# Random features of linear attention as two products of packed, rounded rows, and the second head's outputs behind the next pair's projections

## The chip, the core and the metric

One core of a Trainium2 chip runs the whole program. Its engines run side by side, each with its own queue of instructions: TensorE (PE in the rows; PEld is its weight load) multiplies, VectorE (DVE) and ScalarE (ACT) work element by element on SBUF and PSUM, GpSimd (POOL) and SyncE (SP) issue transfers. They meet at semaphores. The metric is the device time of one execution in microseconds, lower is better.

## The reference

A network of two layers on 1250 tokens of width 768: graph attention and linear attention side by side, then a feed-forward part. The change is in the linear attention, which each layer does once, with 12 heads of width 64. Layer 0 has 384 random features, another set `w` for each head, a bias on q, k and v, and a scale:

```python
def _feature_map(x, w):                       # layer 0, SCALE = 64 ** -0.25
    xs = x * SCALE
    proj = jnp.einsum('bhnc,hcm->bhnm', xs, w)
    sq = 0.5 * jnp.sum(xs * xs, axis=-1, keepdims=True)
    return jnp.exp(proj - sq) / np.sqrt(M)
...
q = _feature_map(qkv[0], w_orf)
k = _feature_map(qkv[1], w_orf)
D = jnp.einsum('bhnm,bhm->bhn', q, jnp.sum(k, axis=2))[..., None] + EPSILON
ktv = jnp.einsum('bhnm,bhnc->bhmc', k, v)
out = jnp.einsum('bhnm,bhmc->bhnc', q, ktv) / D
```

Layer 1 does the same with 256 features that all heads share, no bias and no scale.

## The kernel before

The program is a chain of stages. `performer_stage` is called twice, as `perf0` (layer 0, m = 384 features) and `perf1` (layer 1, m = 256). Tokens come in 10 tiles of 125, the 768 channels in 6 blocks of 128, the 12 heads in 6 pairs, so that a pair's q or k is one 128-row product: rows 0 to 63 are the first head (x = 0), rows 64 to 127 the second (x = 1). The input and the projection weights are split into a high part, rounded to the f32r format, and a rest in the same format; a projection is three f32r products per block (rest by high, high by rest, high by high, L592).

Before the change a pair goes so:

- TensorE projects q, then k (L592), in chunks of 512, 512 and 226 tokens into three PSUM banks. Every second pair it computes the values of two pairs first (L576).
- VectorE adds the bias and copies each chunk to SBUF, one copy per head (L732, without bias L735), and writes the squares of a head's 64 rows into the 64 rows of the other half of the same buffer (L742).
- The feature product (L605) is one plain fp32 product over 128 rows: 64 rows of q or k by the features, 64 rows of squares by the constant -0.5 times the scale. So exp needs no further term. These products go round five PSUM banks, and ScalarE empties them with exp (L672) into `qphi` and `kphi`.
- `k_t_v` (L630) sums kphi by v over the tokens, 65 columns wide with a column of ones for the denominator; VectorE copies the result (`keep_ktv`, L754). `outputs` (L643) is qphi by that, and VectorE divides (`keep_out`, L764 to L769) and SyncE stores.
- TensorE's order for heads 0 and 1: q(0), k(0), k(1), k_t_v(0), q(1), outputs(0), k_t_v(1), outputs(1). Then the next pair is projected.

The order is that of the code, engine by engine; no planner sets it. VectorE has further work in this stage: it splits the next weights (`split_w`, L706 and L708), and in `perf1` it scans one head of the graph attention per pair for its maxima (`MaxScan`, L1708, ten tiles of 125 x 1250), before it looks at the pair's `keep_ktv`. In `perf0` GpSimd adds the graph's edges to a matrix by 160 scattering transfers (L438), beside all this.

## Time and profile before

| | |
|---|---|
| time, median of 3 runs | 3726.37 us (3709.74 to 3729.12) |
| time of the profiled execution | 3719.97 us |
| its span | 3718.2 us |
| mean granted TensorE clock | 0.912 |
| TensorE busy | 3131.9 us, 84% of the span |
| VectorE busy | 2224.0 us, 60% |
| ScalarE busy | 1269.7 us, 34% |
| `perf0` | about 143 to 669 us of the span |
| `perf1` | about 2567 to 3009 us |

The span is what the trace covers; the execution's own time lies 1.8 us above it. The granted clock is the share of full speed that the chip allows TensorE: 1.00 is 2.4 GHz and 0.50 is 1.2 GHz. Matmuls are pipelined, so what one of them costs in a row of them is the distance from start to start, not the duration shown beside it. A plain fp32 product leaves two records in the trace.

### The profile page before, as it was taken

The page shows a single profiled execution, that of the slowest core. Times are in us where ns is not written, and L with a number is a line of the kernel's source. Part 1 is how long each engine was busy: PE and PEld are TensorE (multiplying, and loading weights), DVE is VectorE, ACT ScalarE, POOL GpSimd, SP SyncE. Part 2 cuts the span into 40 slices and gives each one's busy share as a digit, 9 for nine tenths or more (in the row PEclk, how much of TensorE's full clock was granted, in tenths as well). Part 3 has the DMA queues.
Part 4 walks back from the last instruction along what each step waited for, and adds up shares of the span by engine and source line. Part 5 has one row for each costly group of instructions (what it writes and reads, how often), then busy time and mean ns, then how long its engine had stood idle before and what let it go on. Part 6 is the DMA issues. An engine that isn't in the chain of part 4 may idle for free. (4 is left out here: it accounts for less than half of the span.)

```text
span 3718.2 us, 49900 instructions
## 1 busy us (share of the span) xinstructions
PE 3131.9 (84%) x18054; PEld 2553.8 (69%) x18054; DVE 2224.0 (60%) x3569; ACT 1269.7 (34%) x2193; POOL 452.4 (12%) x301
## 2 busy tenths in 40 slices
PE   8799999769899898786978499876999966886695
PEld 5678788655687898675977133356888844776694
DVE  6422222455670454996774788656654647996775
ACT  5341322213111332554133477521211211553245
POOL 0488860110000000000001400000000000000000
PEclk9799999889899999998989599878999988997897
DMA  6222220675420653422331211254111065214121
GB/s 200 56 28 23 24 20 8 194 221 132 107 61 29 175 157 94 125 74 82 76 76 26 82 39 47 60 176 125 39 40 41 14 170 155 70 43 119 47 51 43
DMA packets 253114, 311.06 MB, mean 84 GB/s; under 512 B 98898, under 2 KB 182455, under 8 KB 252297
## 3 DMA queue, kind: packets, MB, share of 16 engines
q1 hardware_dynamic: 178141, 276.25, 27.3%
q0 software_dynamic: 74784, 32.32, 4.9%
q8 instruction: 115, 1.88, 0.2%
q14 instruction: 74, 0.61, 0.1%
HBM read 226.94 MB, written 80.57 MB: 83 GB/s over the span
## 5 line engine op out<-in xcount | busy, mean ns | idle before, releaser
L438 POOL DMA_INDIRECT adj_d<-key_val,key_off x160 | 333.5, 2085 | 193.7 <-issue 166.7
L672 ACT ACTIVATE perf_qphi<-perf_wide,perf_lnm 128x512 f32<-128x512 f32 x180 | 102.9, 605 | 687.0 <-PE perf_wide L605 687.0
L2921 DVE TENSOR_TENSOR expert_wgel<-expert_gel,expert_wps 128x417 f32<-128x417 f32 (+1 forms) x384 | 201.7, 584 | 63.4 <-PE expert_wps L2846 57.8
L1909 PE MATMUL gat00att_ops<-gat00att_h,gat00att_p 125*125 x1600 | 197.3, 279 | 45.9 <-DVE gat00att_p L1885 45.9
L1909 PE MATMUL gat10att_ops<-gat10att_h,gat10att_p 125*125 x1600 | 194.4, 278 | 48.0 <-DVE gat10att_p L1885 47.9
L1909 PEld LDWEIGHTS gat00att_ops<-gat00att_h,gat00att_p 125*125 125x125 f32 x1600 | 183.1, 189 | 60.3 <-issue 60.1
L1909 PEld LDWEIGHTS gat10att_ops<-gat10att_h,gat10att_p 125*125 125x125 f32 x1600 | 182.4, 190 | 60.3 <-issue 60.3
L2893 ACT ACTIVATE expert_gel<-expert_hps 128x417 f32<-128x417 f32 (+1 forms) x384 | 193.5, 519 | 51.3 <-DVE expert_wgel L2921 42.3
L1212 PE MATMUL fc_ops<-fc_w_hi,fc_x_lo 128*125 128x384 f32 x480 | 164.7, 343 | 15.1 <-DVE fc_w_lo L1260 15.1
L1068 PE MATMUL fc_ps<-y_lo,fc_w_hi 128*128 128x512 f32 (+1 forms) x432 | 155.1, 359 | 19.4 <-DVE fc_w_lo L1110 19.4
L903 PE MATMUL proj_hps<-proj_w,proj_aT 128*125 128x384 f32 x480 | 164.3, 501 | 0.6 <-DMA proj_w<-in_L_mix_W_proj 0.3
L1212 PE MATMUL fc_ops<-fc_w_lo,fc_x_hi 128*125 128x384 f32 x480 | 164.1, 342 | 0.0
L592 PE MATMUL perf_wide<-y_lo,perf_qk_hi 128*128 128x512 f32 (+1 forms) x432 | 154.4, 358 | 10.8 <-DVE perf_v L721 10.8
L1212 PE MATMUL fc_ops<-fc_w_hi,fc_x_hi 128*125 128x384 f32 x480 | 163.5, 341 | 0.0
L1068 PE MATMUL fc_ps<-y_hi,fc_w_lo 128*128 128x512 f32 (+1 forms) x432 | 155.4, 360 | 0.0
L1068 PE MATMUL fc_ps<-y_hi,fc_w_hi 128*128 128x512 f32 (+1 forms) x432 | 155.4, 360 | 0.0
L592 PE MATMUL perf_wide<-y_hi,perf_qk_lo 128*128 128x512 f32 (+1 forms) x432 | 154.3, 357 | 0.0
L592 PE MATMUL perf_wide<-y_hi,perf_qk_hi 128*128 128x512 f32 (+1 forms) x432 | 154.1, 357 | 0.0
L2839 PE MATMUL expert_hps<-first_z,first_w 99*128 99x417 bf16 (+1 forms) x384 | 132.1, 348 | 24.0 <-SPq L2794 20.2
L643 PE MATMUL perf_o_ps<-perf_ktv,perf_qphi 128*125 128x65 f32 x1200 | 146.1, 286 | 5.9 <-DVE perf_ktv L754 5.9
L643 PEld LDWEIGHTS perf_o_ps<-perf_ktv,perf_qphi 128*125 128x125 f32 x1200 | 144.9, 202 | 7.6 <-issue 7.5
L1834 ACT ACTIVATE gat10att_e<-gat10att_e,a_s 125x1250 f32<-125x1250 f32 x80 | 107.0, 1338 | 103.8 <-DVE gat10att_e L1872 103.6
(465 smaller groups left out, 7814.8 us busy)
## 6 DMA issues: line engine op xcount, KB each, us to landing
fc_w<-in_L_mix_fc_w SPq DMA_DIRECT2D x96, 384.0 KB
adj_d<-edge_zero SPq DMA_DIRECT2D x4, 2734.4 KB
gat00proj_adj<-adj_d POOLq DMA_DIRECT2D x20, 546.9 KB, 6.9
gat00att_sh<-shift_d SPq DMA_DIRECT2D x16, 546.9 KB
gat10att_sh<-shift_d SPq DMA_DIRECT2D x16, 546.9 KB
perf_w<-in_L_mix_qkv_w SPq DMA_DIRECT2D x18, 384.0 KB
perf_w<-in_L_mix_W_qkv SPq DMA_DIRECT2D x18, 384.0 KB
attn_d<-perf_o SPq DMA_DIRECT2D x12, 560.0 KB
```

Of the source, the lines that this page charges most:

```text
L438: nc.gpsimd.indirect_dma_start(out=adj_flat[u], out_offset=bass.IndirectOffsetOnAxis(ap=key_off[:, c:c + 1], axis=0), in_=key_val[:, c:c + ...
L592: ins = pe.matmul(proj[:, c0:c0 + cn], qk_parts[wp][:, k, kb, :], y_parts[yp][:, kb, c0:c0 + cn], start=(kb == 0 and n == 0), stop=(kb == ...
L643: ins = pe.matmul(o_ps[0:TP, bank, (t - t0) * vw:(t - t0 + 1) * vw], qphi[:, x, mb, t * TP:(t + 1) * TP], ktv[:, x, mb, :], start=(mb == 0 ...
L672: act.activation(out, in_, ACT.Exp, bias=lnm[0:parts, 0:1], scale=scale).then_inc(exp_done, 1)
L903: ins = pe.matmul(hps[0:TP, t % 2, c * 512:c * 512 + 384], aT[:, t % 2, kb, :], w[:, kb, c * 384:(c + 1) * 384], start=(kb == 0), stop=(kb ...
L1068: ins = pe.matmul(ps[:, u, c0:c0 + cn], wp[:, u, kb, :], yT[yp][:, kb, c0:c0 + cn], start=(kb == 0 and n == 0), stop=(kb == KB - 1 and n = ...
L1212: ins = pe.matmul(ops[0:TP, t % 4, c * 512:c * 512 + half], xp[:, u, rows], wp[:, u, c * half:(c + 1) * half], start=(k == 0 and n == 0), ...
L1834: act.activation(e[:, s % RING, :], e[:, s % RING, :], ACT.Exp, bias=a_s02[:, bass.ds(hd, 1), s]).then_inc(e_done, 1)
L1909: ins = pe.matmul(ops[0:TP, u, b, t * w:(t + 1) * w], p[:, s, (t0 + t) * TP:(t0 + t + 1) * TP], h[:, s, bass.ds(hd, 1), :], start=(s == 0 ...
L2839: pe.matmul(hps[:, q % 3, 0:cn], w1[0:ZK, u, j * 128:(j + 1) * 128], z[0:ZK, u, c0:c0 + cn], start=True, stop=True).then_inc(h_done, 1)
L2893: act.activation(gel[:, q % 3, 0:cn], hps[:, q % 3, 0:cn], ACT.Gelu_apprx_tanh).then_inc(gel_done, 1)
L2921: dve.tensor_tensor(wgel[:, q % W, 0:cn], gel[:, q % 3, 0:cn], wps[:, q % 3, 0:cn], ALU.mult).then_inc(wgel_done, 1)
```

## The change

- The feature product becomes two f32r products into the same bank. The first has on its 128 rows the rounded q or k of a head (64 rows) and its rest (64 rows), against the rounded features on both halves (`wa`). The second has the rounded values again, against the rests of the features, and on the other 64 rows the summed squares, rounded, and their rests, against -0.5 (`wb`).
- The packed rows are made in two steps. ScalarE, `rounded`: per chunk two Identity instructions over 64 rows, each of which writes the rounded chunk twice, and four Squares over 32 rows. VectorE, `rests`: per chunk one add of the squares' halves over 96 rows, two subtractions over 64 rows, two casts and two subtractions over 32 rows. VectorE's old copies and squares go.
- Chunks are 418, 416 and 416 tokens. k is projected before q.
- TensorE's order becomes k(0), q(0), k_t_v(0), k(1), outputs(0), k_t_v(1), q(1), a wait for all exps of the pair, every second pair the values, the next pair's projections, and only then outputs(1).
- `kphi` and `qphi` hold one head instead of two, so ScalarE's exps of head 1 wait for k_t_v(0) and outputs(0), and those of the next pair for k_t_v(1) and outputs(1). Outputs start on a third of qphi.
- VectorE's order per pair: split the next weights, four scan tiles, `keep_ktv(0)`, perhaps a split, two scan tiles, `keep_out(0)`, four scan tiles, `keep_ktv(1)`, in `perf0` the features' split, perhaps the values, the next pair's `rests`, `keep_out(1)`.
- The loop does two turns of two pairs, and the last two pairs are written out behind it. Two small buffers of the graph attention are allocated later; their instructions stay the same.

```diff
     mb_n = m // 128
     per = 512 // m
     n_k = NT // per
     n_phi = n_k + 3 * mb_n
-    Q0, K0 = (0, n_k + n_phi), (3 * mb_n, n_phi)
+    units = 2 * n_phi
+    K0, Q0 = (0, n_phi), (n_k, n_phi + n_k)
+    cols = [(0, 418), (418, 416), (834, 416)]
+    widest = 418
     phi_banks = [3, 4, 0, 1, 2]
     ring = len(phi_banks)
...
+                    def feature_bank(j):
+                        if 2 <= j < ring:
+
+                            pe.wait_ge(lo_done, g * 6 + 3 + j - 1)
+                        elif j >= ring:
+                            pe.wait_ge(exp_done, g * units + j - ring + 2)
+                        return phi_banks[j % ring]
+
+                    def k_features(x):
+                        fw = x if per_head else 0
+                        for n in range(n_k):
+                            bank = feature_bank(K0[x] + n)
+                            for y in range(per):
+                                tile = slice((n * per + y) * TP, (n * per + y + 1) * TP)
+                                out = wide[0:TP, bank, y * m:(y + 1) * m]
+                                pe.matmul(out, ab[:, 0, x, 0, tile], wa[:, fw, :], start=True, stop=False)
+                                ins = pe.matmul(out, ab[:, 0, x, 1, tile], wb[:, x, :], start=False, stop=True)
+                            ins.then_inc(phi_done, 1)
+
+                    def q_features(x):
+                        fw = x if per_head else 0
+                        j = Q0[x]
+                        for c, (c0, cn) in enumerate(cols):
+                            if x == 0:
+                                pe.wait_ge(s_done, g * 6 + 3 + c + 3)
+                            for mb in range(mb_n):
+                                bank = feature_bank(j)
+                                f = slice(mb * 128, (mb + 1) * 128)
+                                pe.matmul(wide[:, bank, 0:cn], wa[:, fw, f], ab[:, 1, x, 0, c0:c0 + cn],
+                                          start=True, stop=False)
+                                pe.matmul(wide[:, bank, 0:cn], wb[:, x, f], ab[:, 1, x, 1, c0:c0 + cn],
+                                          start=False, stop=True).then_inc(phi_done, 1)
+                                j += 1
...
+                    if per_head:
+                        pe.wait_ge(feat_split, g + 1)
+
+                    pe.wait_ge(s_done, g * 6 + 5)
+                    k_features(0)
+                    q_features(0)
+                    k_t_v(0)
+                    k_features(1)
+                    outputs(0)
+                    k_t_v(1)
+                    q_features(1)
+                    if not last:
+                        pe.wait_ge(exp_done, g * units + units + 1)
+                        if u == 1:
+                            values(i + 1)
+                        project(g + 1, i + u, 1 - u)
+                    outputs(1)
...
-                        pe.wait_ge(feat_ld[u], i * 32 + 32)
-                        pe.wait_ge(square_done, g * 12 + 6)
-                        q_features(0)
-
-                        pe.wait_ge(square_done, g * 12 + 12)
-                        k_features(0)
-                        k_features(1)
-                        k_t_v(0)
-                        q_features(1)
-                        outputs(0).then_inc(o_done, 1)
-                        k_t_v(1)
-                        outputs(1).then_inc(o_done, 1)
...
+                    for side in range(2):
+                        for c, (c0, cn) in enumerate(cols):
+                            n = side * 3 + c
+                            act.wait_ge(proj_done, g * 6 + n + 1)
+
+                            def bias(k, r0, r1):
+                                return bpair[r0:r1, k, 1 - side:2 - side] if biased else 0.0
+
+                            for x in range(2):
+                                r0 = 64 * x
+                                act.activation(ab[r0:r0 + 64, side, x, :, c0:c0 + cn],
+                                               wide[r0:r0 + 64, c, 0:cn].unsqueeze(1).to_broadcast([64, 2, cn]),
+                                               ACT.Identity, bias=bias(0, r0, r0 + 64))
+
+                            act.wait_ge(s_done, g * 6 + n + 1)
+                            act.wait_ge(add_done, g * 6 + n + 1)
+                            for x in range(2):
+                                r0, to = 64 * x, slice(64 - 64 * x, 96 - 64 * x)
+                                act.activation(sq[to, n % 2, 0:cn], wide[r0:r0 + 32, c, 0:cn], ACT.Square,
+                                               bias=bias(1, r0, r0 + 32), scale=root)
+                                ins = act.activation(more[to, 0:cn], wide[r0 + 32:r0 + 64, c, 0:cn], ACT.Square,
+                                                     bias=bias(1, r0 + 32, r0 + 64), scale=root)
+                            ins.then_inc(sq_done, 1)
...
+                    def k_exps(x):
+
+                        act.wait_ge(ktv_done, g * 2 + x + 1)
...
+                    k_exps(0)
+                    q_exps(0)
+                    k_exps(1)
+                    q_exps(1)
+                    if not last:
+                        rounded(g + 1)
...
-                        q_exps(0)
-                        k_exps(0)
-                        k_exps(1)
-                        q_exps(1)
...
-                        for k, dest in enumerate((qs, ks)):
-                            for c, (c0, cn) in enumerate(CHUNKS):
-                                dve.wait_ge(proj_done, g * 6 + k * 3 + c + 1)
-                                for x in range(2):
-                                    rows = slice(64 * x, 64 * x + 64)
-                                    if biased:
-                                        ins = dve.tensor_scalar(dest[rows, x, c0:c0 + cn], proj[rows, c0:c0 + cn],
-                                                                bcols[rows, bass.ds(g + k * KB, 1)], None, ALU.add)
-                                    else:
-                                        ins = dve.tensor_copy(dest[rows, x, c0:c0 + cn], proj[rows, c0:c0 + cn])
-                                    ins.then_inc(plain_done, 1)
-
-                                dve.wait_ge(plain_done, g * 12 + k * 6 + 2 * c + 2)
-                                for x in range(2):
-                                    rows, other = slice(64 * x, 64 * x + 64), slice(64 - 64 * x, 128 - 64 * x)
-                                    got = dest[rows, x, c0:c0 + cn]
-                                    dve.tensor_tensor(dest[other, x, c0:c0 + cn], got, got, ALU.mult).then_inc(square_done, 1)
-
-                        if u == 0:
-                            split_w(qk_parts, i * 3 + 2)
-                        elif not last:
-                            split_w(v_parts, i * 3 + 3)
-                        if scan is not None:
-
-                            scan.head(dve, g + 1, 0, g + 1)
...
-                        keep_ktv(0)
-                        if u == 1 and not last:
-                            split_w(qk_parts, i * 3 + 4)
-                        keep_out(0)
-                        keep_ktv(1)
-                        keep_out(1)
...
+                    for side in range(2):
+                        for c, (c0, cn) in enumerate(cols):
+                            n = side * 3 + c
+                            at = slice(c0, c0 + cn)
+                            dve.wait_ge(sq_done, g * 6 + n + 1)
+                            dve.tensor_tensor(sq[0:96, n % 2, 0:cn], sq[0:96, n % 2, 0:cn], more[0:96, 0:cn],
+                                              ALU.add).then_inc(add_done, 1)
+                            for x in range(2):
+                                rows, other = slice(64 * x, 64 * x + 64), slice(64 - 64 * x, 128 - 64 * x)
+                                high = ab[rows, side, x, 0, at].bitcast(F32)
+                                if biased:
+                                    ins = dve.scalar_tensor_tensor(
+                                        out=ab[other, side, x, 0, at], in0=wide[rows, c, 0:cn],
+                                        scalar=bpair[rows, 0, 1 - side:2 - side], in1=high,
+                                        op0=ALU.add, op1=ALU.subtract)
+                                else:
+                                    ins = dve.tensor_tensor(ab[other, side, x, 0, at], wide[rows, c, 0:cn], high, ALU.subtract)
+                            ins.then_inc(lo_done, 1)
+                            dve.wait_ge(add_done, g * 6 + n + 2)
+                            for x in range(2):
+                                r = 64 - 64 * x
+                                dve.tensor_copy(ab[r:r + 32, side, x, 1, at], sq[r:r + 32, n % 2, 0:cn]).then_inc(s_high, 1)
+                            for x in range(2):
+                                r = 64 - 64 * x
+                                dve.wait_ge(s_high, (g * 6 + n) * 2 + x + 1)
+                                ins = dve.tensor_tensor(ab[r + 32:r + 64, side, x, 1, at], sq[r:r + 32, n % 2, 0:cn],
+                                                        ab[r:r + 32, side, x, 1, at].bitcast(F32), ALU.subtract)
+                            ins.then_inc(s_done, 1)
...
+                    if not last:
+                        split_w(qk_parts, i * 3 + 2 + 2 * u)
+                    if scan is not None:
+                        scan.start(dve, g + 1, 0, g + 1)
+                        scan.tiles(dve, g + 1, 0, 0, 4)
+                    keep_ktv(0)
+                    if u == 0 and not (isinstance(i, int) and i == HP // 2 - 1):
+                        split_w(v_parts, i * 3 + 3)
+                    if scan is not None:
+                        scan.tiles(dve, g + 1, 0, 4, 6)
+                    keep_out(0)
+                    if scan is not None:
+                        scan.tiles(dve, g + 1, 0, 6, NT)
+                        scan.finish(dve, g + 1, 0)
+                    keep_ktv(1)
+                    if not last:
+                        if biased:
+                            set_bias(g + 1)
+                        if per_head:
+
+                            dve.wait_ge(phi_done, g * units + units)
+                            split_features(g + 1)
+                        if u == 1:
+                            keep_values(i + 1)
+                        rests(g + 1)
+                    keep_out(1)
```

TensorE in `perf0`, before: from the end of the second head's q features of one pair to the first projection of the next (`perf_wide` are the five banks).

```order
L605 MATMUL perf_wide<-perf_qs,perf_feat 128x226
L638 REGISTER_ALU
L639 ISA
L643 MATMUL perf_o_ps<-perf_ktv,perf_qphi 125x65 x30
L630 MATMUL perf_ktv_ps<-perf_v,perf_kphi 128x65 x30
L637 REGISTER_ALU
L638 REGISTER_ALU
L639 REGISTER_ALU
L643 MATMUL perf_o_ps<-perf_ktv,perf_qphi 125x65 x30
L569 ISA
L581 REGISTER_ALU
L592 MATMUL perf_wide<-y_lo,perf_qk_hi 128x512
```

Both outputs (L643) stand ahead of the next projection (L592); nothing but registers stands between k_t_v(1) and outputs(1).

TensorE in `perf0`, after: the end of the q features of head 1 (L632, L634) and the start of the next projection.

```order
L632 MATMUL perf_wide<-perf_ab,perf_wa 128x416
L634 MATMUL perf_wide<-perf_ab,perf_wb 128x416
L674 REGISTER_ALU
L587 ISA
L596 MATMUL perf_wide<-y_lo,perf_qk_hi 128x418
L596 MATMUL perf_wide<-y_hi,perf_qk_lo 128x418
L596 MATMUL perf_wide<-y_hi,perf_qk_hi 128x418
```

And the end of that projection, where outputs(1) now stands, and the next pair's features behind it.

```order
L596 MATMUL perf_wide<-y_hi,perf_qk_hi 128x416
L650 REGISTER_ALU
L651 REGISTER_ALU
L657 MATMUL perf_o_ps<-perf_ktv,perf_qphi 125x65 x9
L655 REGISTER_ALU
L657 MATMUL perf_o_ps<-perf_ktv,perf_qphi 125x65 x21
L663 REGISTER_ALU
L665 REGISTER_ALU
L619 MATMUL perf_wide<-perf_wa,perf_ab 125x384
L620 MATMUL perf_wide<-perf_wb,perf_ab 125x384
```

What moved: the projections of 108 products stand between q(1) and outputs(1), and outputs(1) is cut by a wait for its last exps, which are over by then.

VectorE in `perf1`, before: the end of a pair's ten scan tiles (`perf_sums<-perf_mask,perf_row`), then `keep_ktv(0)` and `keep_out(0)`.

```order
L1708 ISA perf_sums,perf_top<-perf_mask,perf_row 125x1250
L1708 ISA perf_top 125x1
L1711 REGISTER_ALU
L1715 ISA
L1715 COPY mx<-perf_top 125x10
L753 ISA
L754 COPY perf_ktv<-perf_ktv_ps 128x130
L761 ISA
L764 TENSOR_SCALAR perf_den<-perf_o_ps 125x7
```

VectorE in `perf1`, after: the third and fourth scan tile of a pair, then `keep_ktv(0)` and the split of the next values' weights.

```order
L1825 ISA perf_sums,perf_top<-perf_mask,perf_row 125x1250
L1825 ISA perf_top 125x1
L1828 REGISTER_ALU
L842 ISA
L843 COPY perf_ktv<-perf_ktv_ps 128x130
L777 ISA
L778 CAST perf_v_hi<-perf_w 128x1536
L779 REGISTER_ALU
L780 TENSOR_TENSOR perf_v_lo<-perf_w,perf_v_hi 128x1536
```

What moved: `keep_ktv(0)` (L754, now L843) stands behind four scan tiles instead of ten, and six tiles stand behind it.

## Rows read from the trace of the kernel before

**Rows 1.** The page's first part: busy time, share, instructions.
```profile
PE 3131.9 (84%) x18054; PEld 2553.8 (69%) x18054; DVE 2224.0 (60%) x3569; ACT 1269.7 (34%) x2193; POOL 452.4 (12%) x301
```

**Rows 2.** Windows: the two stages, busy time by engine, granted clock, DMA.
```profile
core 0: us, PE busy (x) PEld busy (x) DVE busy (x) ACT busy (x) POOL busy (x), PEclk, DMA share, GB/s
143.00:669.00 526.00, 519.23 (x3084) 431.54 (x3084) 141.65 (x247) 133.91 (x230) 327.88 (x158) 0.96 0.20 22
2567.00:3009.00 442.00, 406.84 (x2532) 355.70 (x2532) 251.25 (x416) 84.93 (x134) 8.14 (x14) 0.95 0.15 40
```

**Rows 3.** Timeline of TensorE, one pair of perf0: start, duration, what, idle before.
```profile
363.37 6.46 PE L605 MATMUL perf_wide<-perf_qs,perf_feat 128*128 128x512 f32 x18
369.67 13.06 PE L605 MATMUL perf_wide<-perf_feat,perf_ks 128*125 128x384 f32 x40
382.57 6.81 PE L630 MATMUL perf_ktv_ps<-perf_v,perf_kphi 125*128 125x65 f32 x60
...
409.47 6.76 PE L643 MATMUL perf_o_ps<-perf_ktv,perf_qphi 128*125 128x65 f32 x60 [0.53 <-DVE perf_ktv L754]
...
436.90 0.60 PE L605 MATMUL perf_wide<-perf_qs,perf_feat 128*128 128x512 f32 x1
```

**Rows 4.** Timeline of TensorE, perf0: neighbours in a projection.
```profile
343.53 0.39 PE L592 MATMUL perf_wide<-y_hi,perf_qk_lo 128*128 128x512 f32 x1
343.76 0.39 PE L592 MATMUL perf_wide<-y_hi,perf_qk_hi 128*128 128x512 f32 x1
```

**Rows 5.** Timeline of TensorE, perf1: one pair's features, and the next's.
```profile
2625.69 4.37 PE L605 MATMUL perf_wide<-perf_qs,perf_feat 128*128 128x512 f32 x12
...
2681.85 4.37 PE L605 MATMUL perf_wide<-perf_qs,perf_feat 128*128 128x512 f32 x12
2686.05 8.80 PE L605 MATMUL perf_wide<-perf_feat,perf_ks 128*125 128x256 f32 x40
2694.69 4.58 PE L630 MATMUL perf_ktv_ps<-perf_v,perf_kphi 125*128 125x65 f32 x40
```

**Rows 6.** Groups by shape, ScalarE: exps, and a cast of 750 elements.
```profile
L672 ACT ACTIVATE perf_qphi<-perf_wide,perf_lnm 128x512 f32<-128x512 f32 x120 | 82.5, 687 | 687.0 <-PE perf_wide L605 687.0
L672 ACT ACTIVATE perf_kphi<-perf_wide,perf_lnm 125x384 f32<-125x384 f32 x120 | 69.6, 580 | 7.4
...
L1490 ACT CAST gat00proj_xT_hi<-gat00proj_tps 128x750 fp32r<-128x750 f32 x10 | 7.8, 778 | 38.0 <-PE gat00proj_tps L1430 38.0
```

**Rows 7.** Timeline of ScalarE, perf0: two exps in a row.
```profile
365.29 1.03 ACT L672 ACTIVATE perf_qphi<-perf_wide,perf_lnm 128x512 f32<-128x512 f32 x2 [0.17 <-PE perf_wide L605]
```

**Rows 8.** Groups by shape, VectorE: squares and bias adds of 64 rows.
```profile
L742 DVE TENSOR_TENSOR perf_ks<-perf_ks 64x512 f32<-64x512 f32 x48 | 33.0, 687 | 1.6
...
L732 DVE TENSOR_SCALAR perf_ks<-perf_wide,perf_bcols 64x512 f32<-64x512 f32 x24 | 18.0, 751 | 16.2 <-PE perf_wide L592 15.8
...
L742 DVE TENSOR_TENSOR perf_ks<-perf_ks 64x226 f32<-64x226 f32 x24 | 9.4, 392 | 0.8
```

**Rows 9.** Timeline of VectorE, perf1: squares, a split, scan tiles, a division.
```profile
2677.30 1.41 DVE L742 TENSOR_TENSOR perf_ks<-perf_ks 64x512 f32<-64x512 f32 x2
...
2684.61 0.96 DVE L706 CAST perf_v_hi<-perf_w 128x1536 fp32r<-128x1536 f32 x1
...
2687.28 1.45 DVE L1708 CUSTOM_DVE_ANT_0 perf_sums<-perf_mask,perf_row 125x1250 bf16<-125x1250 bf16 x1
...
2690.31 1.46 DVE L1708 CUSTOM_DVE_ANT_0 perf_sums<-perf_mask,perf_row 125x1250 bf16<-125x1250 bf16 x1 [0.19 <-DVE perf_top L1708]
...
2708.40 0.89 DVE L769 TENSOR_TENSOR perf_o<-perf_o_ps,perf_rden 125x448 f32<-125x448 f32 x2
```

**Rows 10.** Groups by shape, ScalarE: table loads at the exps.
```profile
L672 ACT ACT_TABLE_LOAD x6 | 7.7, 1283 | 10.9 <-DVE perf_v L701 10.9
```

**Rows 11.** Timeline of TensorE, perf0: outputs(1) of another pair.
```profile
306.37 12.35 PE L643 MATMUL perf_o_ps<-perf_ktv,perf_qphi 128*125 128x65 f32 x60 [0.53 <-DVE perf_ktv L754]
```

**Rows 12.** Windows: that stretch, its granted clock third from the end.
```profile
306.00:318.00 12.00, 11.63 (x58) 11.64 (x59) 0.23 (x1) 0.00 (x0) 9.99 (x5) 0.54 0.16 2
```

More of the change, by code:

```diff
@@ L461, in performer_stage @@
     vw = HD + 1
+    root = float(np.sqrt(scale))
     with Stage(nc, name) as S:
@@ L662, in _ @@
+                        pair(i, u, False)
+                for u in range(2):
+                    pair(HP // 2 - 1, u, u == 1)
             @block.scalar
@@ L786, in _ @@
                     scan.head(dve, 0, 0, 0)
+                keep_values(0)
+                rests(0)
                 with dve.Fori(0, HP // 2 - 1) as i:
-                    pairs(i, False)
-                pairs(HP // 2 - 1, True)
+                    for u in range(2):
+                        pair(i, u, False)
+                for u in range(2):
+                    pair(HP // 2 - 1, u, u == 1)
                 if scan is not None:
```

294 lines of the change are left out of this document (158 added, 136 removed).

## Prediction

> **What bounds the kernel now.** I read the page's first part [rows 1], then the two stages in windows [rows 2], then TensorE's timeline through one pair of each [rows 3 to 5], then what ScalarE and VectorE instructions cost [rows 6 to 10]. The reader is to see that TensorE is the bound in both stages: in `perf0` it is busy 519.2 of 526.0 us, in `perf1` 406.8 of 442.0, while ScalarE has 134 and 85 us and VectorE 142 and 251. In `perf1` VectorE carries the scan, so it is no idle engine there. A pair of `perf0` takes 436.90 - 363.37 = 73.5 us from features to features [rows 3], one of `perf1` 2681.85 - 2625.69 = 56.2 [rows 5]; both hold no values.
>
> **TensorE's work, part by part.** In `perf0` the q features of a head take 369.67 - 363.37 = 6.3 us, the k features of both heads 382.57 - 369.67 = 12.9 [rows 3]: 25.5 per pair. An f32r product of 512 columns costs one step of 0.23 us [rows 4]; by columns, 418 cost 0.19, 384 cost 0.175 and 256 cost 0.12. The new k features are 10 tiles x 2 products x 0.175 = 3.5 per head, the q features 9 x 2 x 0.19 = 3.4, so 13.9 per pair instead of 25.5. In `perf1` it is 4.2 per head for q and 8.6 for k [rows 5], 17.0 per pair, against 2 x (20 x 0.12 + 12 x 0.19) = 9.4. The projection has the same columns in all: 436.90 less the end of outputs(1) (409.47 + 6.76) is 20.7 [rows 3], and stays. A k_t_v or an outputs stays at 6.65 in `perf0`, 4.4 in `perf1` (40 products for 60). If TensorE remained the bound, that would be 11.6 x 6 + 7.6 x 6 = 115 us. Most of it can't be had, for the following reason.
>
> **What ScalarE and VectorE add.** A chunk on ScalarE is two Identity instructions of 836 elements and four Squares of 418. An exp costs 0.687 for 512 elements and 0.580 for 384, a cast of 750 costs 0.778 [rows 6]; the slope of these, 0.00084 per element, puts 836 at 0.96 (the cast's own per-element pace would give 0.85) and 418 at 0.61. That is 2 x 0.96 + 4 x 0.61 = 4.36. Two exps in a row took 1.03 [rows 7]; they are a chunk of 512 and one of 226 tokens, 0.69 and by the slope 0.44, so they overlap by 0.10. With that in four of six places the chunk is 4.0. The ends: 3.75 with overlap everywhere, 4.5 with none and the semaphore's hop; I take 4.0, since ScalarE's own row overlaps. On VectorE a chunk is seven instructions, of 418 elements. A square of 64 rows costs 0.687 for 512 and 0.392 for 226, a bias add out of PSUM 0.751 [rows 8], so 0.55 to 0.65 each, 4.05 in all: VectorE keeps step with ScalarE, a little behind. The two squares at 2677.30 took 1.41, twice 0.69 and a gap [rows 9]: these run from one half of the rows to the other and don't overlap, and all pairs of instructions in `rests` do the same, so I take no overlap there.
>
> The Trainium skill, "VectorE: DVE Perf Modes", section "Two Vector instructions with no wait between them", says that an instruction whose input or output starts in another group of 32 partitions than the last one's is held until all earlier ones are finished. The row above agrees. The page says it of the Vector engine; the first rival below is what happens if ScalarE does the same, for its instructions change halves too.
>
> **perf0, one pair.** Count from the start P of its projections. The first chunk is ready at P + 3.4 (18 x 0.19), ScalarE starts at 3.8 and ends six chunks at 27.8. TensorE ends the projections at 21.3 (20.7 and short waits) and outputs(1), which now stand here, at 28.0. So the six chunks are just covered: this is where the move of outputs(1) pays, 6.65 us of work beside the tail of the rounding. The last rests are a chunk's first half later, about 29, and banks 0 to 2 wait for them. Then 19 exps (10 of 384 at 0.48, 9 of 418 at 0.51, each less the 0.10) take 9.4; TensorE is five banks ahead and starts k_t_v(0) at 36.8, ends it at 43.5. k(1) is paced by exps that had to wait for k_t_v(0): 3.7, to 47.2. outputs(0) to 53.9, k_t_v(1) to 60.5. q(1) and its nine exps, which must end before the next projection, take 5.5: 66.0. That is 7.5 less than 73.5, five times 37.5. The last pair has no projection behind it: q(1) and outputs(1) end near P + 70 instead of 73.5, and before, its outputs(1) ran at half clock, 5.7 more, so 9.2. That is one of two outputs(1) of the six that ran so; the other took 12.35 instead of 6.76 [rows 3, 11], with a granted clock of 0.54 [rows 12]. It stood behind the wait for `keep_ktv(1)`; now f32r work stands in its place. I take 8 for it: 5.6 by the rows, and an estimated 2.4 for the values behind it, which began slow too. The tables: the exps' six table loads of 1.28 us stood off the path, beside 10.9 of waiting [rows 10]; now the 1.28 comes between the rounding and the first exp, in the loop's body, twice: 2.6 lost. Sum: -37.5 - 9.2 - 8 + 2.6 = -52.
>
> **perf1, one pair.** Projections end at 21.0, outputs(1) at 25.4, ScalarE's chunks at 26.6 to 27.8. Five exps of 512 and six of 418 bring k_t_v(0) to 32.1, its end to 36.6, k(1) to 39.0. Now VectorE: its rests end at 31.5, then keep_out(1) (0.89 and two small steps [rows 9], 1.4), the split of weights (2687.28 - 2684.61 = 2.7), four scan tiles (two in 2690.31 - 2687.28 = 3.03 [rows 9], 6.1), and only then keep_ktv(0): done at 42.2. Behind it on VectorE stand the values' split, six tiles, keep_out(0), on TensorE outputs(0). So TensorE waits 3.2 us. outputs(0) to 46.7, k_t_v(1) to 51.2, q(1) with its exps 4.0: 55.2, one less than 56.2. Five such pairs and a last one: -7. Tables +2.6.
> This 3.2 us wait stands between two blocks of 65-column products, the place in which rows 11 and 12 show half clock after a wait of 0.53 us. If the clock falls there, outputs(0) and k_t_v(1) take 12.35/6.7 times as long, 3.9 more each, 7.8 per pair. I take it for four of the five pairs: +31. Sum: -7 + 2.6 + 31 = +27.
> "TensorE: Matmul & The Clock Gate" of the Trainium skill, section "Why this matters for your kernels", advises to leave no idle gaps between bursts of products, which speaks against this order in the same place.
>
> **Sum.** -52 + 27 = -25. Against the profiled execution's own 3720.0 us that is 3695; the median of the runs is 6.4 above that execution, so 3701 for the median.
>
> **Rivals.**
> 1. ScalarE's instructions don't overlap when they change halves: a chunk is 4.5, the six 3 us longer. `perf0` loses 3 on each of five pairs, 16 with the start; in `perf1` VectorE's chain is the later one and 8 are lost. Net about -1: 3725. For it speaks the row of VectorE's squares; against it, that ScalarE's exps overlap, though with no change of halves.
> 2. The clock stays high in `perf1`: then no +31, and net -57: 3669 and at best 3667. For it: `perf1`'s own k_t_v and outputs ran at 4.4 all through the pair shown; against it, that nowhere there stands a wait of 3 us.
> 3. The other side: half clock also takes k_t_v(0), outputs(0) and k_t_v(1) of `perf0`. TensorE waits there too, for the chunks before the features and for exps before each block, and the features that used to keep it dense have shrunk to half. At 5.7 per block and two blocks a pair, 11 per pair and 57 in the stage: net +31, 3757. It decides from 2.5 us per pair over the ten pairs with a successor. Against it: the waits are shorter than 2 us and f32r products stand between. A chunk beyond 4.5 does the same at 6 us for each 0.1.
>
> **Numbers.** The forecast (3680 to 3715 as its own range) 0.47, rival 1 0.20, rival 2 0.17, rival 3 0.16. The range of 3660 to 3745 takes in rivals 1 and 2 and leaves 3, in its half beyond 3745, and the far ends out. What this kernel's measurement can tell from no change is 0.5%, 18.6 us: faster means under 3707.8, which has the most of the forecast (0.40) and rival 2 and a little more, 0.58; slower means over 3745.0, rival 3 and the far end of 1, 0.19; the same 0.23.
>
> **What would show it.** In the profile after: features of `perf0` at 3.5 and 3.4 us where 6.3 stood; ScalarE's chunk at 4.0 (rival 1 at 4.5); a period of 66 in `perf0` and 55 to 63 in `perf1`; idle before outputs(0) of `perf1` with `keep_ktv` as its releaser, about 3; L657 and the k_t_v rows at twice their length there and a granted clock of 0.5 to 0.6 in that stretch (rival 2: none; rival 3: in `perf0` too). The forecast is wrong if the chunk is off by more than 0.3, or if the half clock is in `perf0` or nowhere.

## The result, and the profile after

The changed kernel took 3677.07 us (3675.6 to 3681.78, three runs) against 3726.37: a ratio of 0.9883, with an interval of 0.9836 to 0.993. In a second comparison with more runs (e0 below) the ratio was 0.9928 (0.9903 to 0.9953), so the change is worth about 27 us there (17 to 36), the first comparison shows 49, and the forecast was 25.

The page's first part after the change, to be held against [rows 1]:

```profile
PE 3017.5 (82%) x18054; PEld 2566.6 (70%) x18054; DVE 2341.4 (64%) x3813; ACT 1533.2 (42%) x2623; POOL 456.0 (12%) x301
```

TensorE lost 114 us of busy time, ScalarE gained 264 and VectorE 117. The two stages in windows, from the first to the last product of each, against [rows 2]; the last row is `perf1` before the change between the same bounds, since the window of [rows 2] runs 17 us beyond its last product:

```profile
core 0: us, PE busy (x) PEld busy (x) DVE busy (x) ACT busy (x) POOL busy (x), PEclk, DMA share, GB/s
121.80:599.30 477.50, 444.62 (x3084) 428.58 (x3084) 207.98 (x376) 271.79 (x446) 331.63 (x158) 0.98 0.24 28
2507.20:2947.10 439.90, 399.24 (x2532) 389.98 (x2532) 281.70 (x501) 213.14 (x350) 7.46 (x14) 0.88 0.14 37
...
2567.60:2992.10 424.50, 406.84 (x2532) 355.70 (x2532) 235.02 (x389) 84.93 (x134) 8.14 (x14) 0.97 0.15 40
```

TensorE is now busy 93% of `perf0` and 91% of `perf1` (before: 96% of `perf1`), and the granted clock of `perf1` fell from 0.97 to 0.88. From the traces, one of each kernel, the time from a stage's first to its last product, in us:

| kernel | start of perf0 | perf0 | between | perf1 | after it |
|---|---|---|---|---|---|
| before | 142.9 | 524.3 | 1900.5 | 424.5 | 726.1 |
| after | 121.9 | 477.3 | 1908.1 | 439.7 | 727.9 |
| e0, the same kernel | 136.0 | 476.5 | 1907.7 | 439.7 | 729.0 |
| e1, keep_ktv(0) earlier | 138.8 | 476.5 | 1907.3 | 392.2 | 726.0 |
| e2, outputs(1) first | 133.0 | 504.9 | 1898.2 | 441.7 | 723.9 |
| e3, perf1 of before | 138.4 | 478.5 | 1900.9 | 428.5 | 725.3 |
| e4, no bias on ScalarE | 134.9 | 467.3 | 1908.1 | 430.9 | 725.2 |
| e5, a fifth Square | 135.2 | 495.2 | 1909.9 | 429.8 | 727.4 |
| e6, one feature product | 128.7 | 505.3 | 1914.6 | 446.0 | 727.9 |
| e7, remainders first | 140.6 | 480.8 | 1910.7 | 400.4 | 726.4 |
| e8, q(1) ahead of k_t_v(1) | 133.4 | 470.1 | 1911.5 | 385.6 | 725.0 |

So the change is worth -47 in `perf0` and +15 in `perf1`. A further 21 us of the first pair of traces lie ahead of `perf0`, in a stage that is the same in both kernels, and the stages between took 8 more, also with the same code; the ten traces of changed kernels have 1898 to 1915 there, so nothing shows that the change made them longer. In the trace of before TensorE ran its products ahead of `perf0` at half pace up to 87 us, in the one after at full pace from 14 to 41. This is read from the products: the trace of before has no record of the clock ahead of 88 us. The same two products of `edge_keys`, first before, then after:

```profile
16.69 2.01 PE L225 MATMUL edge_keys<-edge_diag,edge_ones 125*125 125x500 f32 x2
```

```profile
15.93 1.08 PE L225 MATMUL edge_keys<-edge_diag,edge_ones 125*125 125x500 f32 x2
```

One pair of `perf0` after the change, TensorE's rows, of the features only some (start, duration, idle time ahead and its releaser), against [rows 3]:

```profile
384.91 0.46 PE L596 MATMUL perf_wide<-y_lo,perf_qk_hi 128*128 128x416 f32 x1 [0.61 <-DVE perf_ab L820]
...
392.78 6.66 PE L657 MATMUL perf_o_ps<-perf_ktv,perf_qphi 128*125 128x65 f32 x60
...
402.85 0.44 PE L619 MATMUL perf_wide<-perf_wa,perf_ab 128*125 128x384 f32 x1 [1.95 <-DVE perf_ab L820]
...
403.91 0.52 PE L619 MATMUL perf_wide<-perf_wa,perf_ab 128*125 128x384 f32 x1
404.23 0.52 PE L620 MATMUL perf_wide<-perf_wb,perf_ab 128*125 128x384 f32 x1
...
410.03 6.81 PE L644 MATMUL perf_ktv_ps<-perf_v,perf_kphi 125*128 125x65 f32 x60
...
420.26 6.66 PE L657 MATMUL perf_o_ps<-perf_ktv,perf_qphi 128*125 128x65 f32 x60
426.77 6.86 PE L644 MATMUL perf_ktv_ps<-perf_v,perf_kphi 125*128 125x65 f32 x60
...
438.85 0.38 PE L579 MATMUL perf_wide<-perf_v_lo,y_hi 128*125 128x256 f32 x1 [1.73 <-ACT perf_qphi L729]
```

The rows show outputs(1) (L657, 392.78) behind the projections, then the features, with 1.95 us of waiting for the last chunk's subtraction (L820), k_t_v(0), and at the end 1.73 for the last exp. The next pair's k_t_v(0) starts at 498.41 behind 21.4 us of values, so the period is 67.0 here; it is 67.4 and 67.5 behind the k_t_v(0) at 185.20 and 252.63, and 67.5 in the mean of all five.

The two rows at 403.91 and 404.23 show something else: they start 0.32 apart, where 0.175 is the full pace. Behind the wait of 1.95 us some ten products ran at half clock, to 406.8, and k_t_v(0) at 410.03 ran at full clock again. That k_t_v(0) came 68.5 us behind the one ahead (the values taken out), 1.0 more than the mean.

The third pair with a wait in `perf1`:

```profile
2764.12 4.47 PE L657 MATMUL perf_o_ps<-perf_ktv,perf_qphi 128*125 128x65 f32 x40
...
2772.16 0.38 PE L619 MATMUL perf_wide<-perf_wa,perf_ab 128*125 128x256 f32 x1 [1.64 <-DVE perf_ab L825]
...
2775.10 4.58 PE L644 MATMUL perf_ktv_ps<-perf_v,perf_kphi 125*128 125x65 f32 x40
...
2784.77 7.66 PE L657 MATMUL perf_o_ps<-perf_ktv,perf_qphi 128*125 128x65 f32 x40 [2.68 <-DVE perf_ktv L843]
2792.22 8.74 PE L644 MATMUL perf_ktv_ps<-perf_v,perf_kphi 125*128 125x65 f32 x40
...
2805.38 0.38 PE L579 MATMUL perf_wide<-perf_v_lo,y_hi 128*125 128x256 f32 x1 [1.14 <-ACT perf_qphi L729]
```

outputs(0) waits 2.68 us for keep_ktv(0) (L843), and it and k_t_v(1) then take 7.66 and 8.74 instead of the 4.58 of k_t_v(0) ahead of them, which is also what it took before [rows 5]. The window of the stretch has a granted clock of 0.53 (third from the end):

```profile
2785.00:2800.00 15.00, 15.00 (x77) 15.00 (x76) 9.33 (x18) 0.00 (x0) 0.04 (x1) 0.53 0.01 1
```

### The profile page after: what moved, and what is told of

Read it like the earlier page. It is cut to its first block and busy times, and to the rows that moved or that the text cites. A ratio compares the mean times of both kernels' runs of the same rounds, so it can differ in the third digit from the quotient of the medians.

```text
span 3674.9 us, 50549 instructions
## 1 busy us (share of the span) xinstructions
PE 3017.5 (82%) x18054; PEld 2566.6 (70%) x18054; DVE 2341.4 (64%) x3813; ACT 1533.2 (42%) x2623; POOL 456.0 (12%) x301
## 5 line engine op out<-in xcount | busy, mean ns | idle before, releaser
L596 PE MATMUL perf_wide<-y_lo,perf_qk_hi 128*128 128x416 f32 (+1 forms) x432 | 156.0, 361 | 26.4 <-DVE perf_v L802 10.1
L729 ACT ACTIVATE perf_qphi<-perf_wide,perf_lnm 128x416 f32<-128x416 f32 (+1 forms) x180 | 94.6, 637 | 164.1 <-PE perf_wide L634 163.0
L657 PE MATMUL perf_o_ps<-perf_ktv,perf_qphi 128*125 128x65 f32 x1200 | 149.6, 290 | 11.1 <-DVE perf_ktv L843 11.1
L657 PEld LDWEIGHTS perf_o_ps<-perf_ktv,perf_qphi 128*125 128x125 f32 x1200 | 149.3, 207 | 12.2 <-issue 8.1
L644 PE MATMUL perf_ktv_ps<-perf_v,perf_kphi 125*128 125x65 f32 x1200 | 153.7, 293 | 0.0
L644 PEld LDWEIGHTS perf_ktv_ps<-perf_v,perf_kphi 125*128 125x128 f32 x1200 | 153.4, 211 | 0.0
L596 PE MATMUL perf_wide<-y_hi,perf_qk_lo 128*128 128x416 f32 (+1 forms) x432 | 153.2, 355 | 0.0
```

The costliest lines, as they stand in the source:

```text
L596: ins = pe.matmul(wide[:, c, 0:cn], qk_parts[wp][:, 1 - side, kb, :], y_parts[yp][:, kb, c0:c0 + cn], start=(kb == 0 and n == 0), stop=(kb ...
L644: ins = pe.matmul(ktv_ps[:, mb * vw:(mb + 1) * vw], kphi[:, t, mb * 128:(mb + 1) * 128], v[:, t, 2 * u + x, :], start=(t == 0), stop=(t == ...
L657: ins = pe.matmul(o_ps[0:TP, bank, (t - t0) * vw:(t - t0 + 1) * vw], qphi[:, mb, t * TP:(t + 1) * TP], ktv[:, x, mb, :], start=(mb == 0), ...
L729: act.activation(out, in_, ACT.Exp, bias=lnm[0:parts, 0:1], scale=scale).then_inc(exp_done, 1)
```

## The experiments

All start from the changed kernel unless the text says otherwise. Times are in the table above.

**e0: the changed kernel again.**

> The changed kernel once more, with more runs. In the first pair of traces 21 us of the gain lie ahead of the attention of layer 0, in a stage that the change does not touch: its first product of perf0 starts at 121.89 us instead of 142.86, and TensorE runs its steps at half clock for most of that stage before and not after. Theory A (that is the luck of one execution, and the change itself is worth what its two stages show, -47 in perf0 and +15 in perf1, so -32): over five rounds the ratio is near 0.991 (3693 for 3726), and the start of perf0 is at 122 in some executions and at 143 in others, of both kernels. Theory B (the change moves something that the first stage feels, as the place of buffers): 0.988 again, and all executions of this kernel start perf0 near 122.

Measured: 3685.68 us, ratio 0.9928 (0.9903 to 0.9953); before, beside it, 3712.13 over 17 runs that reach from 3692.05 to 3721.53. The same kernel starts `perf0` at 136.0 now and not at 121.9, and the two stages repeat within 1 us. Theory B falls with that. Of the 21 us, 14 are shown to come and go with the execution; for the rest the variants, which start `perf0` at up to 140.6, speak for theory A. Of the kernel before there is one trace, so its own spread isn't shown.

**e1: keep_ktv(0) behind two scan tiles.**

```diff
-                        scan.tiles(dve, g + 1, 0, 0, 4)
+                        scan.tiles(dve, g + 1, 0, 0, 2)
                     keep_ktv(0)
...
-                        scan.tiles(dve, g + 1, 0, 4, 6)
+                        scan.tiles(dve, g + 1, 0, 2, 6)
```

> In perf1 keep_ktv(0) stands behind two scan tiles instead of four, and four tiles instead of two behind it. Theory A (the late keep_ktv(0) makes TensorE wait 2.2 to 2.7 us ahead of outputs(0) in four of five pairs, and that wait brings the half clock of the next two blocks): the wait falls to under 0.5, both blocks run at full clock, the four periods fall from about 62 to 51 or 52, and the kernel gains 40 us on the changed one. Theory B (the clock falls for the thin products as such, the wait is only beside it): the waits go, the blocks stay at half clock in these pairs, the gain is 10 us.

Measured: 3641.0 us, ratio 0.981 (0.9783 to 0.9837), against e0's 0.9928. The same place of the same pair:

```profile
2756.67 4.48 PE L657 MATMUL perf_o_ps<-perf_ktv,perf_qphi 128*125 128x65 f32 x40
...
2767.66 4.58 PE L644 MATMUL perf_ktv_ps<-perf_v,perf_kphi 125*128 125x65 f32 x40
...
2774.48 4.48 PE L657 MATMUL perf_o_ps<-perf_ktv,perf_qphi 128*125 128x65 f32 x40
2778.80 4.63 PE L644 MATMUL perf_ktv_ps<-perf_v,perf_kphi 125*128 125x65 f32 x40
```

outputs(0) has no wait, both blocks run in 4.5 and 4.6, and `perf1` fell by 47.5 us. Theory A holds. Four waits of 2.2 to 2.7 us are 10 of it. Some 34 came back because outputs(0), k_t_v(1) and q(1) behind them were at full clock again. The last 4 lie at the stage's start and in its last outputs(1), which the edit doesn't touch. So two scan tiles of VectorE, 3.03 us [rows 9], had cost 11 us in each of four pairs.

**e2: outputs(1) ahead of the projections.**

```diff
                     q_features(1)
+                    outputs(1)
                     if not last:
...
                         project(g + 1, i + u, 1 - u)
-                    outputs(1)
```

> outputs(1) stands again behind q(1), ahead of the next pair's values and projections; all else as changed. Theory A (the six rounded chunks set when the next features start, 30 us after the projections' start in perf0, and outputs(1) is hidden in that time): every pair gets longer by outputs(1), 6.65 in perf0 and 4.4 in perf1, less up to 2 that its own wait for the exps had cost: +5 and +3 per pair, five pairs each, +40 in all, with as much more idle time ahead of the k features. Theory B (TensorE's own work is the bound and its order does not matter): within 10 us of the changed kernel.

Measured: 3716.82 us, ratio 1.0017 (0.9996 to 1.0037). `perf0` is 28.4 longer, 5.7 per pair, as theory A has it (5 per pair). Its idle time stands where the features begin:

```profile
351.12 0.53 PE L619 MATMUL perf_wide<-perf_wa,perf_ab 128*125 128x384 f32 x1 [3.65 <-DVE perf_ab L820]
...
355.52 0.68 PE L619 MATMUL perf_wide<-perf_wa,perf_ab 128*125 128x384 f32 x1 [3.55 <-DVE perf_ab L820]
...
363.88 6.81 PE L644 MATMUL perf_ktv_ps<-perf_v,perf_kphi 125*128 125x65 f32 x60
```

These two waits are 7.2 us where the changed kernel has one of 1.95: outputs(1) had covered the rest. In `perf1` only 2 us were lost and not 15: in the second to fifth pair k_t_v(0) comes 33.3 to 34.6 us behind the start of the projections instead of 31.5 to 32.1, while VectorE reaches keep_ktv(0) at 40.7 to 40.8 as in the changed kernel (42.2 once). So outputs(0) waits at most 1.2 us and runs at full clock. The gain of the whole change rests on this move: without it the kernel is no faster than before.

Three waits of `perf1` of this kernel also show how loosely the clock hangs on a wait:

```profile
2625.28 4.58 PE L657 MATMUL perf_o_ps<-perf_ktv,perf_qphi 128*125 128x65 f32 x40 [2.12 <-DVE perf_ktv L843]
...
2671.00 4.55 PE L657 MATMUL perf_o_ps<-perf_ktv,perf_qphi 128*125 128x65 f32 x40 [1.08 <-DVE perf_ktv L843]
```

```profile
2767.36 8.12 PE L657 MATMUL perf_o_ps<-perf_ktv,perf_qphi 128*125 128x65 f32 x40 [2.12 <-DVE perf_ktv L843]
```

The same wait of 2.12 us for the same releaser was followed once by a block of 4.58 and once by one of 8.12.

**e3: perf1 as before.** The stage's old function is called for layer 1.

> Layer 0 has the changed attention, layer 1 the one of before. If the stages are independent, perf1 takes 424 us as before instead of 440, so 15 us less than the changed kernel, and perf0 stays at 477. If the clock or buffers of one stage carry over to others, the difference is another one.

Measured: 3677.71 us, ratio 0.9913 (0.9888 to 0.9939). `perf1` took 428.5, 11 less than changed; the ratio is 0.0015 better than e0's, inside both intervals. Expected were 15 less: the same code took 424.5 in the trace of before and 428.5 here, so 4 us of a stage are within what one trace can show. `perf0` stayed at 478.5. The stages are independent as far as this shows.

**e4: no bias in ScalarE's instructions.** `bias()` returns 0.0.

> On the changed kernel: ScalarE leaves out the bias of q and k in layer 0 (its six instructions per chunk have no bias operand), so their output is another; perf1 is untouched. By the rows of perf1, where there is no bias, a chunk falls from 4.40 to 3.85 us. Theory A (the six chunks are what the next features wait for in perf0): each pair starts its k_t_v(0) up to 3.3 us earlier, less where TensorE's own 7 us of features become the bound; perf0 takes 14 to 19 us less than 476.5. Theory B (VectorE's chunk, 4.0 to 4.4, or TensorE set the pace): under 5 us.

Measured in one execution (3668.57 us): `perf0` 467.3, so -9.2 against e0, between the two theories. The chunk was 3.85, 400.04 to 403.89:

```profile
400.04 1.74 ACT L710 ACTIVATE perf_ab<-perf_wide 64x832 fp32r<-64x832 f32 x2
...
403.89 1.73 ACT L710 ACTIVATE perf_ab<-perf_wide 64x832 fp32r<-64x832 f32 x2
...
409.51 1.05 ACT L729 ACTIVATE perf_kphi<-perf_wide,perf_lnm 125x384 f32<-125x384 f32 x2 [1.81 <-PE perf_wide L620]
```

After the chunks ScalarE had to wait 1.81 us here for TensorE's features, and 1.4 to 2.8 in every other pair behind the first, so TensorE became the bound in part. The five periods fell by 2.7, 0.0, 0.7, 1.9 and 2.6 us against e0, of the 3.3 that six chunks lost. In the second, the features started 30.8 us behind the projections' start, as in e0 (31.0), although the chunks ended 2.6 earlier: they waited for something else. In the third, the one of the rows above, the projections ran at half clock for a stretch and took 23.1 us, against 21.1 in the pair before the values.

**e5: a fifth Square per chunk.**

> On the changed kernel, perf0 only: a fifth Square per chunk, whose result goes to a spare buffer, from the same rows to the same rows as the one ahead of it. Theory A (ScalarE lets an instruction overlap the last one by 0.10 only when both start in the same rows, which rival 1 assumed): it starts 0.51 us behind the fourth and costs about 0.5 per chunk; Theory B (Squares and Identities never overlap, whatever their rows): 0.61 from start to start. For the time both say the same: 6 x 0.5 to 0.6 on the path of each of five pairs and the start, +17 to +22 in perf0 (prediction: 3 us per 0.1 of a chunk in one stage, +15 to +18). If VectorE were the pace, it would be nothing.

```profile
400.65 1.92 ACT L711 ACTIVATE perf_ab<-perf_wide,perf_bpair 64x832 fp32r<-64x832 f32 x2
...
404.41 0.60 ACT L721 ACTIVATE perf_more<-perf_wide,perf_bpair 32x416 f32<-32x416 f32 x1
404.92 0.59 ACT L724 ACTIVATE perf_spare<-perf_wide,perf_bpair 32x416 f32<-32x416 f32 x1
405.54 1.91 ACT L711 ACTIVATE perf_ab<-perf_wide,perf_bpair 64x832 fp32r<-64x832 f32 x2
```

Measured in one execution (3699.74 us): `perf0` 495.2, +18.7 for chunks of 4.89 (400.65 to 405.54), 3.8 us per 0.1. The periods grew by 3.6, 2.0, 2.5, 5.0 and 2.9 us, for chunks that are 2.9 longer per pair; in the first and the fourth of these the features ran at half clock for a stretch, which they did not in e0. The fourth Square starts where the third ended; the fifth, from and to the same rows as the fourth, starts 0.51 behind it, while those that read from other rows than the one ahead start 0.61 behind it. This is so in all 36 places of the trace. Theory A holds: ScalarE does overlap, but not across a change of rows; a change of the rows read is enough. The Trainium skill, "VectorE: DVE Perf Modes", section "Two Vector instructions with no wait between them", states such a rule of the Vector engine alone; this case's rows show the like of it on ScalarE.

**e6: one feature product.** The second product of each pair, with the rests of the features and the squares, is left out.

> On the changed kernel, both stages: the second of the two f32r feature products (rests of the features, squares) is left out, so TensorE has half of the feature work. Theory A (as the working of the prediction has it, TensorE's features are no longer on the path ahead of k_t_v(0) and at the pair's end, where ScalarE paces them; only k(1) between k_t_v(0) and outputs(0) is): 1.8 us per pair in perf0, 11 in all, next to nothing in perf1, where outputs(0) waits for keep_ktv(0) anyway. Theory B (TensorE's work is the bound as before): 7.0 per pair in perf0, 4.7 in perf1, 70 in all.

Measured in one execution (3724.63 us): `perf0` 505.3 and `perf1` 446.0, 29 and 6 us slower, though a pair of `perf0` has 7.0 us less of products:

```profile
408.38 6.66 PE L654 MATMUL perf_o_ps<-perf_ktv,perf_qphi 128*125 128x65 f32 x60
...
418.04 1.55 PE L619 MATMUL perf_wide<-perf_wa,perf_ab 128*125 128x384 f32 x6 [2.24 <-DVE perf_ab L817]
...
424.02 12.90 PE L641 MATMUL perf_ktv_ps<-perf_v,perf_kphi 125*128 125x65 f32 x60
...
440.37 6.66 PE L654 MATMUL perf_o_ps<-perf_ktv,perf_qphi 128*125 128x65 f32 x60
446.87 6.86 PE L641 MATMUL perf_ktv_ps<-perf_v,perf_kphi 125*128 125x65 f32 x60
```

```profile
424.00:437.00 13.00, 13.00 (x62) 12.99 (x62) 0.25 (x2) 1.94 (x4) 8.41 (x5) 0.50 0.59 116
```

Both theories fell. k_t_v(0) of `perf0` now takes 12.90 at a granted clock of 0.50 in four of the six pairs (348.25, 424.02, 520.61, 594.84), where the changed kernel has 6.81 in all six. In `perf1` it takes 8.63 instead of 4.58 in all six, and in the last three outputs(0) and k_t_v(1) are at half clock too. This is the mechanism of the prediction's third rival: half clock in the thin blocks of `perf0`. The changed kernel stands close to it: its features also fall to half clock behind the wait (403.91 above), but are at full clock again before k_t_v(0) starts; with half of the products they are not, in four pairs of `perf0`. That the second products as such keep it away is the nearest reading of this one execution, and no more. The one pair of `perf0` with both k_t_v(0) at full clock (190.58 to 258.14) has a period of 67.6, so fewer products on TensorE gained nothing there either, though its features too ran at half clock for a stretch.

**e7: VectorE's subtractions first, on e1.** The add of the squares stands behind the two subtractions of a chunk.

> The kernel with two scan tiles ahead of keep_ktv(0), and in addition VectorE makes a chunk's two subtractions ahead of the add of the squares. Banks come free 0.6 us earlier per chunk (lo_done), the squares' sums 0.0 later in all. If the last chunk's lo_done is what the features wait for (rows: TensorE waits 1.95 us for it in perf0, 1.63 in perf1), a pair gains 0.6, both stages 6 us: 3635 beside 3641. If ScalarE now waits for the later add (its next Squares need the buffer), the chunk grows by up to 0.1 and the gain is gone or negative.

Measured: 3653.49 us, ratio 0.9834 (0.9805 to 0.9863), against e1's 0.981 (0.9783 to 0.9837): not better. The second branch of the expectation is what happened: ScalarE's next Square waits for the add, a chunk is 4.51 (399.97 to 404.48) instead of 4.40, `perf0` +4.3, `perf1` +8.2. To start the subtractions beside the Squares was not tried.

```profile
399.97 1.92 ACT L710 ACTIVATE perf_ab<-perf_wide,perf_bpair 64x832 fp32r<-64x832 f32 x2
402.01 0.60 ACT L718 ACTIVATE perf_sq<-perf_wide,perf_bpair 32x416 f32<-32x416 f32 x1
...
404.48 1.92 ACT L710 ACTIVATE perf_ab<-perf_wide,perf_bpair 64x832 fp32r<-64x832 f32 x2
```

**e8: q(1) ahead of k_t_v(1), on e1.**

```diff
                     outputs(0)
+                    q_features(1)
                     k_t_v(1)
-                    q_features(1)
```

> The kernel with two scan tiles ahead of keep_ktv(0), and in addition TensorE does q(1) ahead of k_t_v(1) in both stages, so that the nine (six) exps of q(1) run beside k_t_v(1) and the projections needn't wait for them. Rows of the changed kernel: that wait is 1.73 to 1.75 us per pair in perf0 and 0.8 to 1.4 in perf1, and ScalarE's next chunk hangs on the projections' start alone. Theory A (the wait is on the path of each pair): the period falls by 1.7 in perf0 and about 1.2 in perf1, 8 and 6 us in all: perf0 468, perf1 386, time 3627 beside 3641. Theory B (the six chunks and their features set the period from some earlier point, as the end of the exps of the pair): no gain. Side effect to look for: k_t_v(1) and the projections still stand apart from outputs(0) by dense products, so no new half clock is expected.

Measured: 3626.89 us, ratio 0.9755 (0.9722 to 0.9788). `perf0` 470.1 and `perf1` 385.6, 6.4 and 6.6 less than e1; expected were 8 and 6. The exps of q(1) run beside k_t_v(1), and the projections start without a wait. This is the fastest version, faster than both kernels; its interval just overlaps e1's, and the 13 us between the two are read from one trace each.

## Why the prediction was right

**Direction and size.** -25 was forecast, -32 is what the two stages show, and e0 measured -27. The split was right in kind: -52 forecast and -47 found in `perf0`, +27 and +15 in `perf1`. Both parts were off, by 5 and by 12, and as the errors have opposite signs, the sum is closer than its parts: that is luck in part. The first comparison's 3677.07 is 24 below the forecast's 3701 and just outside its own 3680 to 3715; only the wider range of 3660 to 3745 holds it. It lies near rival 2's 3669 without rival 2's mechanism, for `perf1` did run at half clock. The further 22 us of the first comparison are mostly the state of the clock in an earlier stage; the forecast had no term for it, and no reading of the diff could give one.

**The mechanism, by the prediction's own signs.** The shorter features (3.6 us for k, 3.4 to 3.9 for q), the half clock in `perf1` with `keep_ktv` as the releaser of the wait, and the cover by outputs(1) came as described. But the prediction calls itself wrong if the chunk is off by more than 0.3, and in `perf0` it is off by 0.4. It also does so for half clock in `perf0`: there is some, on features (some ten products from 403.6 us in the pair above), though on none of the blocks that rival 3 named.

**The chunk on ScalarE (4.0).** Mis-sized, in both directions: 4.40 in `perf0`, 3.85 in `perf1`. One chunk of `perf0`, 378.48 to 382.88:

```profile
378.48 1.92 ACT L710 ACTIVATE perf_ab<-perf_wide,perf_bpair 64x832 fp32r<-64x832 f32 x2
380.41 0.60 ACT L718 ACTIVATE perf_sq<-perf_wide,perf_bpair 32x416 f32<-32x416 f32 x1
...
382.88 1.91 ACT L710 ACTIVATE perf_ab<-perf_wide,perf_bpair 64x832 fp32r<-64x832 f32 x2
```

No overlap takes place between instructions that change rows, so rival 1's mechanism is the true one: the prediction's own sum without overlap, 4.36, was right for `perf0`, and the 0.10 that it took off four times was the error. It didn't come at rival 1's price for two reasons. In `perf1` the instructions have no bias operand, which costs 0.09 per instruction: the costs that the forecast took as its base were of exps, which have one (`perf_lnm`, [rows 6]). The groups by shape after the change have both kinds:

```profile
L710 ACT ACTIVATE perf_ab<-perf_wide,perf_bpair 64x832 fp32r<-64x832 f32 x48 | 45.7, 951 | 0.9
L710 ACT ACTIVATE perf_ab<-perf_wide 64x832 fp32r<-64x832 f32 x48 | 41.3, 861 | 0.9
...
L718 ACT ACTIVATE perf_sq<-perf_wide,perf_bpair 32x416 f32<-32x416 f32 x48 | 28.8, 600 | 0.6
...
L718 ACT ACTIVATE perf_sq<-perf_wide 32x416 f32<-32x416 f32 x48 | 24.4, 509 | 0.6
```

In `perf0` the rest of the period was worked out too long, as follows.

**The period of perf0 (66.0).** It is 67.4 to 67.5: the chunks' end moved from 27.8 to 30.1 after the projections' start, 2.3 later, and the rest of the pair took 0.9 less than worked out, so 1.4 us reached the period, 7 us in five pairs. Where nothing else falls in, six chunks that are 3.3 us shorter (e4) take up to 2.7 from a period, and 2.9 longer (e5) add 2.0 to 2.9, so rival 1's 3 us of period for 3 of chunks was nearly right; the sums of the stage give 17 and 38 us per us of chunk, where rival 1 had 32. The whole of `perf0` by terms, from one projection's start to the next: the five pairs with a successor gave 40 us (forecast 43, with the 8 for half clock and values and the tables), the last pair 7.5 (forecast 9.2). That outputs(1) covers the chunks' tail (e2) and that the exps at the pair's end stand on the path (e8) were as worked out.

**perf1: the wait (3.2) and the half clock (+31).** Waits of 2.2 to 2.7, half clock behind four of five, as forecast, e1 being the proof of both; the half clock cost 34. The four disturbed periods are 61.3 to 63.5 (forecast 63.0). The undisturbed one is 51.2 (forecast 55.2, of which 3.2 were the wait). Against five periods of 56.2 that is +19.8 (five periods sum to 300.8). The forecast had five waits of 3.2, 16 us, where four are 10. The values, with what they wait, took 24.9 beyond a period in `perf1` of before (2694.69 to 2775.83 less 56.2) and take 21.4 now, 7 less for two such places, which the forecast did not count. The disturbance is not the same in each execution: in e4 and e5, whose `perf1` is untouched, three pairs of four were at half clock and the stage took 430 and not 440.

**Table loads (+2.6 per stage).** Two per stage after the change, as forecast. No experiment took them away, so their price is not shown; in e0's `perf0` k_t_v(0) of the two pairs with a load comes 39.3 and 39.6 us behind the projections' start, and 38.3 to 38.6 in the other four, which leaves 1.3 each at most.

**Rival 3** didn't come, but e6 shows that it was no idle fear: with half of the feature products its price was 29 us in `perf0`, half of the 57 worked out, since only one block per pair fell, in four of six pairs.

## What to carry to other kernels

Ask of each wait on TensorE what runs behind it: here 10 us of waiting cost 44, since thin fp32 products behind a wait ran at half clock, and moving two scan tiles on another engine took it all back. Taking products away from TensorE can make it slower (e6, one execution). When work moves to an engine whose instructions change rows each time, count them without overlap and with their operands, and look for a block that can stand beside them: here that move was the whole gain.

## What the runs showed of the hardware

- Two Squares of 416 on ScalarE, from and to the same rows, overlap by 0.10 us (0.51 from start to start, e5); where the rows read change, they don't (0.61).
- A bias operand out of SBUF costs ScalarE 0.09 us per instruction: 0.600 and 0.509 for the same Square, 0.951 and 0.861 for the same Identity.
- The first stage ran at half pace up to 87 us in one execution and at full pace from 14 to 41 in another of a kernel with the same code there; `perf0` started at 122 to 143 us in eleven traces. The kernel before had a median of 3726.37 over three runs and of 3712.13 over seventeen.
- An equal wait of 2.12 us was followed by full clock once and by half clock once. What decides between them is left open.
- Half clock also falls on f32r products: some ten of 384 columns started 0.32 us apart behind a wait of 1.95 us, where 0.175 is the full pace.
